# Layer 2's cross attention: who turns the outputs of its heads and their result

## The chip, the cores and the metric

One core of one Trainium2 chip runs the whole program. The metric is device time in microseconds (us), from one launch to its end. Below, PE is TensorE (PEld its weight loads), DVE is VectorE, ACT is ScalarE, POOL is GpSimd, and SP issues the DMAs.

## What is computed

Twelve blocks in four layers (cross attention, attention, feed-forward in each) add to `x`, 64 sequences of 64 tokens with 128 features. The block that changes is the first one of layer 2 (called L2x). Its queries come from `x` and its keys and values from a context of 64 x 128 tokens with 96 features:

```python
def _L2_xattn_ref(query, key_value, Wq, bq, Wk, bk, Wv, bv, Wo, bo):
    NUM_HEADS, CLAMP = 16, 10000.0
    ...
    q = (query @ Wq + bq).reshape(B, Nq, H, D).transpose(0, 2, 1, 3)
    k = (key_value @ Wk + bk).reshape(B, Nkv, H, D).transpose(0, 2, 1, 3)
    v = (key_value @ Wv + bv).reshape(B, Nkv, H, D).transpose(0, 2, 1, 3)
    attn = jnp.einsum('bhqd,bhkd->bhqk', q, k) * scale
    attn = jnp.clip(attn, -CLAMP, CLAMP)
    attn = jax.nn.softmax(attn, axis=-1)
    x = jnp.einsum('bhqk,bhkd->bqhd', attn, v).reshape(B, Nq, Cq)
    return x @ Wo + bo
...
x = x + _L2_xattn_ref(_layernorm(x, axis=-1), ctx_768, ...)
```

## The kernel before

`x` stays in SBUF through all blocks. Each block is cut into jobs of 512 tokens (L1x and L2f: 256), and two contexts, 0 and 1, work on one job each at a time. Each context has four PSUM banks, its own tiles and its own semaphores. `PLAN` says which jobs a context runs one after the other; L2x has eight jobs, four to a context.

A job is written as small programs, one or several for each engine, that yield between steps. `ORDER` is a string of some 8,300 letters; each letter lets one program of one context take its next step (a small letter is context 0, a capital context 1). `write_out` walks through it, so `ORDER` fixes the sequence of instructions on every engine, and each engine runs its own list strictly in turn. A digit in `ORDER` tells the next step to put so many filler products (`pe_warm`, L471, a 128x128 by 128x512 bf16 product whose result nobody reads) on TensorE ahead of a wait. The wait of an instruction is on semaphores that other engines raise.

A job of L2x goes like this. `pe_context`, `act_context` and `dve_L2x` make the keys (L1875, moved with bias by L1898), four masked copies of them in `kx` (two by VectorE at L1761, two by GpSimd at L2032), the values `va` (L1880, L2055), and the queries (normalised tokens turned at L463, moved at L479, multiplied at L1890, moved at L480). The values have a 17th kind of column: for each head a column of ones beside its 8 features, so that the product with the weights also gives their sum.

Then two lanes, h = 0 and 1, take eight heads each, with two of the context's four banks each. A lane makes four waves (w), each of two sequences:

1. L1969, PE: scores of 128 queries against 8 x 128 keys, in the lane's two banks.
2. L2074, L2077, L2080, DVE: maximum, its clamp, and the scores less the maximum, to `p`.
3. L2013, L2015, ACT: a Relu and the exponential, on `p`.
4. L1977, PE: eight turns of 128x128, back to the lane's banks. L2018, ACT: copy to `pT`.
5. L1985, PE: 16 products of weights and values, whose nine rows for each head land in the partitions 32n to 32n+8 of the lane's first bank.
6. L2022, ACT: copy of these 128x256 outputs to `oT`. L1992, PE: two 128x128 turns of `oT` into the lane's second bank.
7. L2083, L2086, DVE: reciprocal of the sums and the product with it, from that bank to `att`. The next wave's scores wait for this (`att`).

```python
            yield
            pe_warm(nc, j, 2 * h + 1)
            t.wait_ge(*j.at(lane_name("outT", h), w + 1))
            for g in groups:
                put = t.transpose(psum[:, 2 * h + 1, (g % 2) * P:(g % 2 + 1) * P], m["oT"][:, 0, g * P:(g + 1) * P], j.c["ident"])
            put.then_inc(*j.up(lane_name("o_turned", h)))
```

So four lanes are under way at once, two for each context, and there are 64 lane waves in all. After both lanes of a job are done, `att` (128 tokens x 128 features, four tiles) is turned by four 128x128 turns (L463), copied to `xT` (L479), multiplied by `Wo` (`pe_project`, L1387) and added to `x` (`dve_project`, L1394), which frees the context's banks (`done`).

Blocks L1a and L3x already turn their outputs in another way: `dve_divide` has VectorE turn blocks of 32x32 straight from PSUM (L1744), divide (L1747, L1750) and turn blocks again into `xT` (L1755).

## Time and profile before

| what | value |
|---|---|
| median of three runs | 2608.11 us (2601.25 to 2614.97) |
| the profiled execution's own time | 2616.77 us |
| its span | 2615.5 us |
| its mean granted TensorE clock | 0.963 of full speed |
| PE busy | 2331.4 us, 89% |
| DVE busy | 1702.6 us, 65% |
| ACT busy | 1340.3 us, 51% |
| POOL busy | 780.3 us, 30% |

Times of single instructions come from the profiled execution, which took 8.7 us longer than the median of the runs. Busy time of an engine counts each moment once, whereas the busy time of a group sums its instructions; a group's line shows the line of the kernel, engine, operation, output and inputs with their shapes, the count, the busy time and the mean, and then for how long the engine had stood idle just before these instructions and what ended that. PE busy includes the fillers and the overlap of pipelined products, so it says little by itself. The stage of L2x reaches from its first scores at 981 us to its last projection at 1288 us.

### The profile page before, as it was taken

What the parts mean: (1) busy time and instruction counts of PE and PEld (TensorE: products, weight loads), DVE (VectorE), ACT (ScalarE), POOL (GpSimd) and SP (SyncE); (2) the same over time, 40 slices, a digit from 0 to 9 for tenths busy, and PEclk for the clock granted to TensorE, in tenths of its full rate; (3) what the DMA queues carried; (4) which work ended last, traced back from release to release, by engine and by line L of the source; (5) the groups of instructions that cost most, each with busy time, mean ns of one, the idle gap of its engine ahead of it and who ended that gap; (6) DMA issues with size and microseconds to landing.
All of it is one profiled execution on the core that took longest, in us unless ns stands there. A gap on an engine that the chain in (4) does not pass through costs nothing.

```text
span 2615.5 us, 62549 instructions
## 1 busy us (share of the span) xinstructions
PE 2331.4 (89%) x26728; PEld 1560.2 (60%) x26728; DVE 1702.6 (65%) x4776; ACT 1340.3 (51%) x2305; POOL 780.3 (30%) x684
## 2 busy tenths in 40 slices
PE   5899999888889998888898888889989888999999
PEld 2566666665545555555576667666645555566666
DVE  4866556667887667768676776666776665655432
ACT  3576445776344338777754444444433566555342
POOL 2322555554121331111012233321210112454434
PEclk8999999999899999999999999999998899999999
DMA  4001442000000000000000000010010000122323
GB/s 124 14 1 37 100 105 60 22 15 11 3 3 6 1 23 37 14 14 2 11 15 19 18 19 19 27 31 14 26 55 8 8 2 2 49 53 53 106 73 89
DMA packets 50454, 84.18 MB, mean 32 GB/s; under 512 B 9536, under 2 KB 24768, under 8 KB 49792
## 3 DMA queue, kind: packets, MB, share of 16 engines
q1 hardware_dynamic: 50176, 80.18, 11.1%
q8 instruction: 210, 3.44, 0.5%
q14 instruction: 68, 0.56, 0.1%
HBM read 77.54 MB, written 2.62 MB: 31 GB/s over the span
## 4 chain that ended last, share of the span: by engine, by line
PE 55%; DVE 22%; ACT 11%; POOL 5%; issue 4%; DMA 2%; SPq 1%; DVEq 0%; POOLq 0%; ACTq 0%
PE psum L938 6%; PE psum L896 5%; PE psum L900 5%; PE psum L1598 3%; PE psum L463 2%; DVE c_L3x_most L1718 2%; PE psum L1691 2%; ACT c_L2x_p L2015 2%; PE psum L471 2%; ACT c_L2x_p L2013 2%; PE psum L1588 1%; PE psum L1387 1%; PE psum L765 1%; PE psum L770 1%; PE psum L1437 1%
## 5 line engine op out<-in xcount | busy, mean ns | idle before, releaser
L471 PE MATMUL psum<-halves_held 128*128 128x512 bf16 x616 | 177.6, 402 | 4.1 <-DVE x_held L635 2.2
L885 POOL TENSOR_TENSOR c_L3f_h<-c_L3f_h,c_L3f_spread 128x512 f32<-128x512 f32 x96 | 120.6, 1283 | 140.6 <-DMA c_L3f_spread<-scratch 107.2
L928 DVE TENSOR_TENSOR c_L3f_h<-c_L3f_h,psum 128x512 f32<-128x512 f32 (+1 forms) x112 | 75.6, 685 | 106.0 <-PE psum L900 77.9
L914 ACT ACTIVATE c_L3f_h<-psum 128x512 f32<-128x512 f32 x112 | 64.7, 594 | 108.2 <-PE psum L896 89.2
L938 PEld LDWEIGHTS psum<-weights,c_L3f_h 128*128 128x128 f32 (+1 forms) x896 | 106.7, 192 | 19.8 <-issue 16.0
L938 PE MATMUL psum<-weights,c_L3f_h 128*128 128x128 f32 (+1 forms) x896 | 109.9, 277 | 1.4 <-POOL c_L3f_h L885 1.4
L471 PEld LDWEIGHTS psum<-halves_held 128*128 128x128 bf16 x616 | 56.1, 101 | 85.1 <-issue 42.1
L896 PE MATMUL psum<-c_L3f_xT,weights 128*128 128x512 f32 x208 | 105.0, 596 | 0.0
L900 PE MATMUL psum<-c_L3f_xT,weights 128*128 128x512 f32 x208 | 104.8, 594 | 0.0
L885 POOL TENSOR_TENSOR c_L0f_h<-c_L0f_h,c_L0f_spread 128x512 f32<-128x512 f32 x64 | 80.5, 1276 | 78.3 <-DVE c_L0f_h L928 50.0
L1598 PE MATMUL psum<-c_L3x_qx,c_L3x_kT 32*128 32x256 f32 x512 | 78.8, 428 | 23.2 <-DVE c_L3x_most L1718 15.7
L2074 DVE TENSOR_REDUCE c_L2x_mx<-psum 128x8 f32<-128x1024 f32 x64 | 77.8, 1220 | 25.6 <-PE psum L1969 25.1
L885 POOL TENSOR_TENSOR c_L2f_h<-c_L2f_h,c_L2f_spread 128x256 f32<-128x256 f32 x64 | 46.4, 748 | 140.2 <-DMA c_L2f_spread<-scratch 132.8
L1977 PE MATMUL psum<-constants_held,c_L2x_p 128*128 128x128 f32 x512 | 67.7, 276 | 15.1 <-ACT c_L2x_p L2015 14.9
L2032 POOL TENSOR_TENSOR c_L2x_kx<-c_L2x_kT,constants_held 128x1024 f32<-128x1024 f32 x16 | 31.2, 1968 | 163.6 <-ACT c_L2x_kT L1898 163.6
L1718 DVE TENSOR_REDUCE c_L3x_most<-psum 128x16 f32<-128x2048 f32 x32 | 73.0, 2281 | 10.7 <-PE psum L1588 10.3
L1977 PEld LDWEIGHTS psum<-constants_held,c_L2x_p 128*128 128x128 f32 x512 | 56.5, 141 | 38.4 <-issue 25.4
L2080 DVE SCALAR_TENSOR_TENSOR c_L2x_p<-psum,c_L2x_mx 128x1024 f32<-128x1024 f32 x64 | 77.9, 1222 | 1.3
L1707 ACT ACTIVATE c_L3x_pT<-psum 128x1024 f32<-128x1024 f32 x64 | 62.5, 1021 | 25.8 <-PE psum L1620 25.6
L1598 PEld LDWEIGHTS psum<-c_L3x_qx,c_L3x_kT 32*128 32x128 f32 x512 | 47.0, 197 | 47.5 <-DVE c_L3x_most L1718 26.6
L2013 ACT ACTIVATE c_L2x_p<-c_L2x_p 128x1024 f32<-128x1024 f32 x64 | 67.7, 1058 | 14.4 <-DVE c_L2x_p L2080 14.2
L938 PEld LDWEIGHTS psum<-weights,c_L0f_h 128*128 128x128 f32 x512 | 62.5, 192 | 15.4 <-issue 12.7
(639 smaller groups left out, 6602.2 us busy)
## 6 DMA issues: line engine op xcount, KB each, us to landing
c_L0f_spread<-scratch SPq DMA_DIRECT2D x64, 256.0 KB, 5.3
c_L3f_spread<-scratch SPq DMA_DIRECT2D x32, 512.0 KB, 5.6
c_L2f_spread<-scratch SPq DMA_DIRECT2D x64, 128.0 KB, 3.0
c_L3f_spread<-scratch SPq DMA_DIRECT2D x64, 128.0 KB, 6.1
c_L0x_ctxT<-ctxT SPq DMA_DIRECT2D x8, 384.0 KB, 4.8
c_L1x_ctx<-ctx SPq DMA_DIRECT2D x16, 192.0 KB, 2.4
c_L2x_ctxT<-ctxT SPq DMA_DIRECT2D x8, 384.0 KB, 3.6
c_L3x_ctxT<-ctxT SPq DMA_DIRECT2D x8, 384.0 KB, 3.5
```

Source lines behind the costliest of these rows:

```text
L471: nc.tensor.matmul(j.psum[:, bank, :], j.half["ident"], j.half["take"], start=True, stop=True)
L885: nc.gpsimd.tensor_tensor(h, h, j.m["spread"][:, f, :], ALU.mult).then_inc(*j.up("mixed"))
L896: t.matmul(psum[:, 1 + 2 * f % 3, 0:j.tok], j.weight("gate")[:, cols], m["xT"][:], start=True, stop=True).then_inc(*j.up("gate"))
L900: t.matmul(psum[:, 1 + (2 * f + 1) % 3, 0:j.tok], j.weight("up")[:, cols], m["xT"][:], start=True, stop=True).then_inc(*j.up("inner"))
L928: nc.vector.tensor_tensor(h, h, j.psum[rows, bank, 0:j.tok], ALU.mult).then_inc(*j.up("gated"))
L938: put = nc.tensor.matmul(j.psum[:, 0, k * P:(k + 1) * P], j.m["h"][rows, f, k * P:(k + 1) * P], j.weight("down")[rows, f * P:(f + 1) * P], ...
L1598: nc.tensor.matmul(j.psum[rows, g, at:at + 256].rearrange("p (j q) -> p j q", j=QUAD), j.m["kT"][f, s * keys:(s + 1) * keys], j.m["qx"][f, ...
L1718: put = v.tensor_reduce(m["most"][:, u, :].rearrange("p (g j) -> p g j", j=QUAD), psum[:, :, u * QUAD * keys:(u + 1) * QUAD * keys].rearra ...
L1977: put = t.transpose(psum[:, n // 4, (n % 4) * P:(n % 4 + 1) * P], m["p"][:, n * P:(n + 1) * P], j.c["ident"])
L2013: s.activation(p, p, ACT.Relu, scale=-1.0).then_inc(*j.up(lane_name("e_low", h)))
L2074: v.tensor_reduce(mx, s, AX, ALU.max).then_inc(*j.up(lane_name("max", h)))
L2080: v.scalar_tensor_tensor(p, s, -limit, bcast(mx, 2, SC), ALU.max, ALU.subtract).then_inc(*j.up(lane_name("low", h)))
```

## The change

In L2x the steps 6 and 7 are written in another way, as in `dve_divide`:

- ScalarE's copy (L2022) and TensorE's two turns (L1992) of each lane wave go. VectorE turns the 128x256 outputs in 32x32 blocks from PSUM into `oT` (new L2075), and the reciprocal and the product now read `oT`.
- The products of weights and values (new L1984) write each sequence's 64 columns as two pieces of 32, so that a block turn puts each token where it belongs.
- At the end of a job TensorE's four turns of `att` and ScalarE's copy of them go. VectorE turns `att` (128x512) in 32x32 blocks into `xT` (new L2047). The rows of `Wo` are laid out to match (`by_lane`).
- The next wave's scores wait for `o_turned` in place of `att`.
- In `pe_linear` of L2a, TensorE also waits for the `done` of the context's job before (`free_bank`).
- All of `ORDER` is new; `PLAN` is as it was.

```diff
--- before.py
+++ after.py
@@ -113,7 +113,7 @@
         ("lb", P, 512, lambda a: a["L1_ffn_lora_B"].transpose(0, 2, 1).reshape(P, 512))]
     t["L2x"] = [
         ("wq", P, P, lambda a: a["L2_xattn_Wq"]), ("wk", CX, P, lambda a: a["L2_xattn_Wk"]),
-        ("wv", CX, P, lambda a: a["L2_xattn_Wv"]), ("wo", P, P, lambda a: a["L2_xattn_Wo"]),
+        ("wv", CX, P, lambda a: a["L2_xattn_Wv"]), ("wo", P, P, lambda a: by_lane(a["L2_xattn_Wo"])),
         ("bq", P, 1, lambda a: col(a["L2_xattn_bq"])), ("bk", P, 1, lambda a: col(a["L2_xattn_bk"])),
         ("bv", P, P, lambda a: row(a["L2_xattn_bv"])), ("bo", P, P, lambda a: row(a["L2_xattn_bo"]))]
     t["L2a"] = [
@@ -650,6 +650,8 @@
             put = t.matmul(psum[:, bank, n * P:(n + 1) * P], m["xT"][:, n * P:(n + 1) * P], j.weight(w), start=True, stop=True)
         put.then_inc(*j.up("keys"))
     yield
+    if heads == 16:
+        j.free_bank(t)
     pe_warm(nc, j, 3)
     t.wait_ge(*j.at("values", 1))
     t.wait_ge(*j.at("kx", 1))
@@ -1938,12 +1940,8 @@
     t, m, psum = nc.tensor, j.m, j.psum
     yield from pe_context(nc, j)
     yield
-    t.wait_ge(*j.at("att", j.tiles))
-    t.wait_ge(*j.at("att_b", j.tiles))
-    pe_turn(nc, j, 0, m["att"])
-    yield
-    pe_warm(nc, j, 2)
-    t.wait_ge(*j.at("features", 2))
+    pe_warm(nc, j, 1)
+    t.wait_ge(*j.at("mixed", 1))
     pe_project(nc, j, 2, m["xT"])
 
 
@@ -1956,8 +1954,8 @@
         for w in range(j.tiles):
             yield
             if w:
-                pe_warm(nc, j, 2 * h)
-                t.wait_ge(*j.at(lane_name("att", h), w))
+                pe_warm(nc, j, 2 * h + 1)
+                t.wait_ge(*j.at(lane_name("o_turned", h), w))
             else:
                 t.wait_ge(*j.at("q_ready", 1))
                 t.wait_ge(*j.at("va", 1))
@@ -1982,24 +1980,16 @@
                 for r in range(2):
                     for n in range(QUAD):
                         col = (QUAD * g + n) * P + r * S
-                        put = t.matmul(psum[LANE * n:LANE * n + ONE, 2 * h, (g % 2) * P + r * S:(g % 2) * P + (r + 1) * S],
-                                       m["va"][:, 2 * w + r, QUAD * g + n, :], m["pT"][:, col:col + S], start=True, stop=True)
+                        out = psum[LANE * n:LANE * n + ONE, 2 * h, r * P:(r + 1) * P].rearrange("p (b c) -> p b c", b=2)
+                        put = t.matmul(out[:, :, (g % 2) * LANE:(g % 2 + 1) * LANE], m["va"][:, 2 * w + r, QUAD * g + n, :],
+                                       m["pT"][:, col:col + S].rearrange("p (b c) -> p b c", b=2), start=True, stop=True)
             put.then_inc(*j.up(lane_name("out", h)))
-            yield
-            pe_warm(nc, j, 2 * h + 1)
-            t.wait_ge(*j.at(lane_name("outT", h), w + 1))
-            for g in groups:
-                put = t.transpose(psum[:, 2 * h + 1, (g % 2) * P:(g % 2 + 1) * P], m["oT"][:, 0, g * P:(g + 1) * P], j.c["ident"])
-            put.then_inc(*j.up(lane_name("o_turned", h)))
 
     return program
 
 
 def act_L2x(nc, j):
     yield from act_context(nc, j)
-    yield
-    nc.scalar.wait_ge(*j.at("turned", 2))
-    act_turned(nc, j, j.m["xT"][:], 0).then_inc(*j.up("features"))
 
 
 def act_lane_L2x(h):
@@ -2017,9 +2007,6 @@
             s.wait_ge(*j.at(lane_name("p_turned", h), w + 1))
             s.copy(m["pT"][:, h * 1024:(h + 1) * 1024].rearrange("p (a b) -> p a b", a=2),
                    psum[:, 2 * h:2 * h + 2, :]).then_inc(*j.up("pT1" if h else "pT0"))
-            yield
-            s.wait_ge(*j.at(lane_name("out", h), w + 1))
-            s.copy(m["oT"][:, 0, 256 * h:256 * h + 256], psum[:, 2 * h, 0:256]).then_inc(*j.up(lane_name("outT", h)))
 
     return program
 
@@ -2054,6 +2041,10 @@
     v.wait_ge(*j.at("values", 1))
     v.tensor_tensor(m["va"][:, :, :, 0:WIDTH], psum[:, 2:4, :].rearrange("p a (s h d) -> p (a s) h d", s=4, h=HEADS),
                     bcast(j.weight("bv").rearrange("p (h d) -> p h d", h=HEADS), 1, j.seqs), ALU.add).then_inc(*j.up("va"))
+    yield
+    v.wait_ge(*j.at("att", j.tiles))
+    v.wait_ge(*j.at("att_b", j.tiles))
+    v.transpose(m["xT"][:], m["att"][:].rearrange("p t d -> p (t d)")).then_inc(*j.up("mixed"))
     yield
     v.wait_ge(*j.at("biased", 1))
     dve_project(nc, j, 2)
@@ -2067,7 +2058,8 @@
         p = m["p"][:, h * 1024:(h + 1) * 1024].rearrange("p (n k) -> p n k", k=SC)
         s = psum[:, 2 * h:2 * h + 2, :].rearrange("p a (n k) -> p (a n) k", k=SC)
         mx, z = m["mx"][:, h * 8:(h + 1) * 8], m["z"][:, 0, h * 8:(h + 1) * 8]
-        out = psum[:, 2 * h + 1, 0:256].rearrange("p (h e) -> p h e", h=8)
+        out = m["oT"][:, 0, 256 * h:256 * h + 256]
+        blocks = out.rearrange("p (b g c) -> p b g c", b=4, g=2)
         for w in range(j.tiles):
             yield
             v.wait_ge(*j.at(lane_name("scores", h), w + 1))
@@ -2079,12 +2071,16 @@
             v.wait_ge(*j.at(lane_name("max", h), 2 * w + 2))
             v.scalar_tensor_tensor(p, s, -limit, bcast(mx, 2, SC), ALU.max, ALU.subtract).then_inc(*j.up(lane_name("low", h)))
             yield
+            v.wait_ge(*j.at(lane_name("out", h), w + 1))
+            v.transpose(out, psum[:, 2 * h, 0:256]).then_inc(*j.up(lane_name("o_turned", h)))
+            yield
             v.wait_ge(*j.at(lane_name("o_turned", h), w + 1))
-            v.reciprocal(z, out[:, :, WIDTH]).then_inc(*j.up(lane_name("denom", h)))
+            v.reciprocal(z, lane_blocks(out)[:, :, WIDTH]).then_inc(*j.up(lane_name("denom", h)))
             yield
             v.wait_ge(*j.at(lane_name("denom", h), w + 1))
-            v.tensor_tensor(m["att"][:, w, 64 * h:64 * h + 64].rearrange("p (h d) -> p h d", h=8), out[:, :, 0:WIDTH],
-                            bcast(z, 2, WIDTH), ALU.mult).then_inc(*j.up(lane_name("att", h)))
+            att = m["att"][:, w, :].rearrange("p (b h g d) -> p b h g d", b=4, h=2, g=2)[:, :, h]
+            v.tensor_tensor(att, blocks[:, :, :, 0:WIDTH], bcast(z.rearrange("p (b g) -> p b g", b=4), 3, WIDTH),
+                            ALU.mult).then_inc(*j.up(lane_name("att", h)))
 
     return program
 
@@ -2844,76 +2840,75 @@
 ORDER = (
-    "qQddDDpdDlLdkqddDKDpdVPavagpAlGdPapAgppPvvDaAvkvDvpPaPLqdGQpDadPdKlpVVgaApgVppvvdVaVPAPvQkGADvvpPapDgAqdPaddDGPLplDKPaVV"
...
+    "qQDdDdDdpLldDkqdKQDVpvPadaDgDpPaAgpALpGpPvdvlaAvGdvvpPakgPqpPdaDdKpVVdaApgVlpVVPPApDAGDPvvDadkvAGLvvpPapDgqdPQadpPaKpVdV"
...
```

`by_lane` and `free_bank` were there before:

```python
def by_lane(w):
    return np.ascontiguousarray(w.reshape(4, 4, 8, w.shape[1]).transpose(1, 0, 2, 3)).reshape(P, w.shape[1])
...
    def free_bank(self, engine):
        if not self.first:
            self.free(engine)
```

What the new `ORDER` makes of the lists is best seen in three places. First TensorE where both contexts pass from their second to their third job of L2x. L1387 (now L1389) is a job's projection, L1875 and L1880 (now L1877 and L1882) the keys and values of the next, L1969 (L1967) scores, L1977 (L1975) the turns of `p`, L1985 (L1984) weights by values. Before:

```order
L463 MATMUL psum<-constants_held,c_L2x_att 128x128 x8
L471 MATMUL psum<-halves_held 128x512 x3
L1387 MATMUL psum<-weights,c_L2x_xT 128x128 x4
L1875 MATMUL psum<-c_L2x_ctxT,weights 128x512 x2
L1880 MATMUL psum<-weights,c_L2x_ctxT 128x128 x8
L463 MATMUL psum<-constants_held,c_L2x_xn 128x128 x4
L1387 MATMUL psum<-weights,c_L2x_xT 128x128 x4
L1875 MATMUL psum<-c_L2x_ctxT,weights 128x512 x2
L471 MATMUL psum<-halves_held 128x512
L1890 MATMUL psum<-c_L2x_xT,weights 128x512
L1880 MATMUL psum<-weights,c_L2x_ctxT 128x128 x8
```

And now:

```order
L1389 MATMUL psum<-weights,c_L2x_xT 128x128 x4
L1984 MATMUL psum<-c_L2x_pT,c_L2x_va 9x2x32 x16
L471 MATMUL psum<-halves_held 128x512
L1967 MATMUL psum<-c_L2x_kx,c_L2x_qT 64x512 x4
L471 MATMUL psum<-halves_held 128x512
L1975 MATMUL psum<-constants_held,c_L2x_p 128x128 x8
L1984 MATMUL psum<-c_L2x_pT,c_L2x_va 9x2x32 x16
L471 MATMUL psum<-halves_held 128x512 x3
L1967 MATMUL psum<-c_L2x_kx,c_L2x_qT 64x512 x4
L1877 MATMUL psum<-c_L2x_ctxT,weights 128x512 x2
L1882 MATMUL psum<-weights,c_L2x_ctxT 128x128 x8
L471 MATMUL psum<-halves_held 128x512
```

Before, the two projections stood four rows of the list apart, with the keys and values of the one between them; now they stand fifteen rows apart, and between them the other context's lanes go on (the second projection is four rows below this piece). Counted over the stage, the pairs stand 12, 4 and 12 rows apart before and 29, 15 and 30 now; the last pair is one row of eight products in both.

Second, VectorE in the middle of a job, where L2083 and L2086 are now L2078 and L2082, L2074, L2077 and L2080 are L2066, L2069 and L2072, and L2075 is new. Before:

```order
L2083 RECIPROCAL c_L2x_z<-psum 128x8
L2086 TENSOR_TENSOR c_L2x_att<-psum,c_L2x_z 128x64
L2074 TENSOR_REDUCE c_L2x_mx<-psum 128x8
L2077 TENSOR_SCALAR c_L2x_mx<-c_L2x_mx 128x8
L2080 SCALAR_TENSOR_TENSOR c_L2x_p<-psum,c_L2x_mx 128x1024
L2083 RECIPROCAL c_L2x_z<-psum 128x8
L2086 TENSOR_TENSOR c_L2x_att<-psum,c_L2x_z 128x64
L2074 TENSOR_REDUCE c_L2x_mx<-psum 128x8
L2077 TENSOR_SCALAR c_L2x_mx<-c_L2x_mx 128x8
```

And now:

```order
L2072 SCALAR_TENSOR_TENSOR c_L2x_p<-psum,c_L2x_mx 128x1024
L409 TENSOR_SCALAR c_L2x_norm_rstd<-c_L2x_norm_moments 128x4
L2075 STREAM_TRANSPOSE c_L2x_oT<-psum 128x256
L2078 RECIPROCAL c_L2x_z<-c_L2x_oT 128x8
L2082 TENSOR_TENSOR c_L2x_att<-c_L2x_oT,c_L2x_z 128x4x16
L2066 TENSOR_REDUCE c_L2x_mx<-psum 128x8
L2069 TENSOR_SCALAR c_L2x_mx<-c_L2x_mx 128x8
L2072 SCALAR_TENSOR_TENSOR c_L2x_p<-psum,c_L2x_mx 128x1024
```

The pair of reciprocal and product has become three instructions, with the block turn at their head, and it stands between the subtraction of one lane and the maximum of another, as it did.

Third, TensorE's fillers (L471) within the lanes. Before:

```order
L1985 MATMUL psum<-c_L2x_pT,c_L2x_va 9x64 x16
L471 MATMUL psum<-halves_held 128x512 x7
L1977 MATMUL psum<-constants_held,c_L2x_p 128x128 x8
L1985 MATMUL psum<-c_L2x_pT,c_L2x_va 9x64 x16
L471 MATMUL psum<-halves_held 128x512
L1977 MATMUL psum<-constants_held,c_L2x_p 128x128 x8
L1992 MATMUL psum<-constants_held,c_L2x_oT 128x128 x4
L1985 MATMUL psum<-c_L2x_pT,c_L2x_va 9x64 x32
```

And now:

```order
L471 MATMUL psum<-halves_held 128x512 x3
L1967 MATMUL psum<-c_L2x_kx,c_L2x_qT 64x512 x4
L471 MATMUL psum<-halves_held 128x512 x9
L1975 MATMUL psum<-constants_held,c_L2x_p 128x128 x8
L471 MATMUL psum<-halves_held 128x512 x4
L1975 MATMUL psum<-constants_held,c_L2x_p 128x128 x8
L1984 MATMUL psum<-c_L2x_pT,c_L2x_va 9x2x32 x16
L471 MATMUL psum<-halves_held 128x512 x2
L1967 MATMUL psum<-c_L2x_kx,c_L2x_qT 64x512 x4
```

The rows with L1992 are gone, and rows of fillers stand ahead of most turns and scores. From the first to the last row of L2x there were 187 fillers and are now 315; outside it there were 429 and are 408. Apart from what is named above, the number and the forms of the instructions are the same on every engine.

## Rows read from the trace of the kernel before

**Rows 1.** Windows: stretch, its length, then busy us and (count) of each engine, clock.
```profile
core 0: us, PE busy (x) PEld busy (x) DVE busy (x) ACT busy (x) POOL busy (x), PEclk, DMA share, GB/s
981.00:1288.00 307.00, 271.55 (x3645) 158.58 (x3645) 225.86 (x416) 242.98 (x317) 43.65 (x29) 0.99 0.04 14
1000.00:1040.00 40.00, 36.88 (x591) 21.40 (x579) 31.10 (x58) 37.92 (x53) 0.00 (x0) 1.00 0.01 2
1120.00:1140.00 20.00, 18.27 (x195) 12.54 (x183) 7.72 (x22) 9.18 (x14) 7.71 (x4) 1.00 0.14 41
1140.00:1150.00 10.00, 8.37 (x42) 3.68 (x42) 9.84 (x21) 6.68 (x8) 3.22 (x4) 0.83 0.00 0
600.00:800.00 200.00, 168.25 (x3444) 105.46 (x3443) 158.46 (x382) 89.95 (x168) 50.25 (x38) 0.92 0.02 4
```

**Rows 2.** Groups by line, VectorE, 980 to 1290 us: count, busy us, mean ns, idle before.
```profile
L2074 DVE TENSOR_REDUCE c_L2x_mx<-psum 128x8 f32<-128x1024 f32 x64 | 77.8, 1220 | 25.6 <-PE psum L1969 25.1
...
L2086 DVE TENSOR_TENSOR c_L2x_att<-psum,c_L2x_z 128x64 f32<-128x64 f32 x64 | 13.5, 220 | 1.3
L2083 DVE RECIPROCAL c_L2x_z<-psum 128x8 f32<-128x8 f32 x64 | 12.6, 201 | 38.6 <-PE psum L1992 37.9
```

**Rows 3.** Groups by line, ScalarE, the same stretch.
```profile
L2022 ACT COPY c_L2x_oT<-psum 128x256 f32<-128x256 f32 x64 | 22.8, 368 | 8.2 <-PE psum L1985 7.7
...
L479 ACT COPY c_L2x_xT<-psum 128x512 f32<-128x512 f32 x15 | 8.6, 585 | 16.6 <-PE psum L463 16.6
```

**Rows 4.** Groups by line, TensorE, the same stretch.
```profile
L471 PE MATMUL psum<-halves_held 128*128 128x512 bf16 x187 | 53.9, 392 | 1.9 <-DVE c_L2x_p L2080 1.9
...
L1992 PE MATMUL psum<-constants_held,c_L2x_oT 128*128 128x128 f32 x128 | 25.5, 291 | 5.3 <-ACT c_L2x_oT L2022 4.8
...
L463 PE MATMUL psum<-constants_held,c_L2x_att 128*128 128x128 f32 x32 | 4.9, 282 | 2.1 <-DVE c_L2x_att L2086 1.9
```

**Rows 5.** The chain of waits, 1000 to 1040 us, shares by line.
```profile
by line: ACT c_L2x_p L2015 21.2%; ACT c_L2x_p L2013 19.3%; ACT c_L2x_pT L2018 16.0%; ACT c_L2x_xn L424 7.7%; PE psum L1969 7.6%; PE psum L1977 7.5%; PE psum L1985 6.8%; ACT c_L2x_oT L2022 4.2%; PE psum L471 4.0%; PE psum L1992 3.5%; issue 1
```

**Rows 6.** One line each, VectorE: min/median/max ns, first and last start, form.
```profile
L1744 DVE STREAM_TRANSPOSE c_L3x_oT<-psum x32: 682/717/718, 1787.3 to 2186.8; 128x512 f32<-128x512 f32 x32
L1744 DVE STREAM_TRANSPOSE c_L1a_oT<-psum x16: 1207/1250/1251, 654.8 to 833.5; 128x1024 f32<-128x1024 f32 x16
...
L1755 DVE STREAM_TRANSPOSE c_L3x_xT<-c_L3x_att x32: 254/311/313, 1788.6 to 2188.2; 128x128 f32<-128x128 f32 x32
L1755 DVE STREAM_TRANSPOSE c_L1a_xT<-c_L1a_att x16: 431/445/446, 659.1 to 835.6; 128x256 f32<-128x256 f32 x16
```

**Rows 7.** One line each, TensorE: products of weights and values.
```profile
L1691 PE MATMUL psum<-c_L3x_pT,c_L3x_va x2048: 218/219/315, 1786.1 to 2186.5; 128*9 128x64 f32 x187
...
L1985 PE MATMUL psum<-c_L2x_pT,c_L2x_va x2048: 218/219/226, 993.4 to 1284.9; 128*9 128x64 f32 x187
```

**Rows 8.** Timeline, the end of one lane's wave: start us, duration us, engine, line.
```profile
1163.85 0.63 PE L1985 MATMUL psum<-c_L2x_pT,c_L2x_va 128*9 128x64 f32 x32
...
1164.55 0.37 ACT L2022 COPY c_L2x_oT<-psum 128x256 f32<-128x256 f32 x1
...
1164.97 0.44 PE L1992 MATMUL psum<-constants_held,c_L2x_oT 128*128 128x128 f32 x2 [0.17 <-ACT c_L2x_oT L2022]
...
1165.45 0.21 DVE L2083 RECIPROCAL c_L2x_z<-psum 128x8 f32<-128x8 f32 x1 [1.27 <-PE psum L1992]
```

**Rows 9.** Timeline, the end of a job, 1201 to 1205 us.
```profile
1201.73 0.35 DVE L2086 TENSOR_TENSOR c_L2x_att<-psum,c_L2x_z 128x64 f32<-128x64 f32 x2
...
1202.23 0.63 PE L463 MATMUL psum<-constants_held,c_L2x_att 128*128 128x128 f32 x4 [0.78 <-DVE c_L2x_att L2086]
1202.89 0.58 ACT L479 COPY c_L2x_xT<-psum 128x512 f32<-128x512 f32 x1
...
1203.53 1.16 PE L1387 MATMUL psum<-weights,c_L2x_xT 128*128 128x128 f32 x8 [0.68 <-ACT c_L2x_xT L479]
```

**Rows 10.** Timeline, a run of five filler products.
```profile
1170.76 1.24 PE L471 MATMUL psum<-halves_held 128*128 128x512 bf16 x5
```

137 lines of the change are left out of this document (68 added, 69 removed).

## The prediction

> **What bounds the kernel now.** I read first where the stage that changes lies and how full each engine is in it. L2x takes 307 us, from 981 to 1288 us of the span. In it ScalarE is busy for 243.0 us (79%), VectorE for 225.9 us (74%) and TensorE for 271.6 us (88%), its fillers included [rows 1]. No engine is full over the whole stage, but the stage has two kinds of stretches. While all four lanes run, as from 1000 to 1040 us, ScalarE is busy for 37.92 of 40 us, 94.8%, and VectorE for 31.10, 78% [rows 1]. The chain of waits says the same there: its largest shares are ScalarE's Relu, exponential and copy of `pT` (19.3, 21.2 and 16.0%); the copy that the change removes has 4.2% and TensorE's turns of it 3.5% [rows 5]. Where both contexts pass to their next job at nearly the same time, as from 1120 to 1140 us, ScalarE is busy for 9.2 of 20 us and VectorE for 7.7 [rows 1]: the time goes to projection, keys and queries. So L2x is bound by ScalarE with holes at the changes of jobs.
>
> Next I read what the steps to be removed cost their engines, and who waits at them. The copies of the outputs are 64 x 368 ns, 22.8 us on ScalarE; those of the result and of the tokens together are 15 in the window, 585 ns each [rows 3]. TensorE's turns of the outputs are 25.5 us, those of `att` 4.9 us [rows 4]. VectorE has stood idle for 38.6 us ahead of the 64 reciprocals, nearly all of it until those turns had ended, and for 25.6 us ahead of the maxima [rows 2]. That is the room into which new work on VectorE can go without lengthening anything.
>
> **The change, part by part.** *ScalarE* loses 22.8 us, and 8 copies of 585 ns, 4.7 us [rows 3]. It keeps 243.0 - 27.5 = 215.5 us.
>
> *VectorE* gains two kinds of turns, and L2x has neither now. The trace has such turns in other blocks: from PSUM, 128x512 takes 717 ns and 128x1024 takes 1250 ns (medians), from SBUF 128x128 takes 311 and 128x256 takes 445 ns [rows 6]. From PSUM an element costs (1250 - 717)/512 = 1.04 ns, so 128x256 should take 717 - 266 = 451 ns, and 64 of them 28.9 us. From SBUF it is (445 - 311)/128 = 1.05 ns, so 128x512 should take 445 + 268 = 713 ns, and 8 of them 5.7 us. The bounds for the first are 311 ns (as small as the smallest turn there is) and 717 ns (as long as the next larger one): 20 to 46 us. I take the value on the line, since two rows of the same form give it. The reciprocals (201 ns) and products (220 ns) [rows 2] read SBUF in place of PSUM and keep their sizes; I change nothing there. VectorE then needs 225.9 + 34.6 = 260.5 us. It becomes the fullest of the three beside TensorE, and is about where ScalarE is now with 243.0.
>
> The Trainium skill, in VectorE: DVE Perf Modes, section The TRN2 errata, gives an operation from PSUM on VectorE 120 cycles and one for each element, at 0.96 GHz; for 256 elements that would be 392 ns and an estimated 25.1 us in place of 28.9, and the stage below would come out some 4 us shorter. For 512 elements it would give 658 ns where the row has 717, so the row decides.
>
> *TensorE* loses 25.5 + 4.9 = 30.4 us [rows 4]. It gets 128 more fillers in the stage (315 against 187). In a run they take 1.24 us for five [rows 10], so some 0.21 to 0.25 us each once one has begun, and 53.9/187 = 0.29 us by the group's line [rows 4]: 27 to 37 us. That is the same room again. Where they stand ahead of a wait that lasts anyway they cost nothing; the cover is ScalarE's Relu and exponential, or VectorE's steps. If that cover were gone they would cost their own length (a rival, below). The products of weights by values write two pieces of 32 columns; L3x, which does so now, has a median of 219 ns as has L2x [rows 7], so 0.
>
> *The path of one lane* grows shorter. The last output of a wave is done at 1164.48 us; copy, hand-over and turns bring the reciprocal to 1165.45 us, 0.97 us later [rows 8]. With a hand-over of 0.07 us, as the copy has, a turn of 0.45 us and 0.03 us to the next instruction it would be 0.55 us: 0.42 us less, and a lane has 16 waves, 6.7 us. At the end of a job the last product ends at 1202.08 us and the projection starts at 1203.53 us, 1.45 us [rows 9]; a turn of 0.71 us and a hand-over take 0.8: 0.6 us less, four times in a context, 2.5 us. Together 9 us, if nothing queued anywhere. What is queued behind the new turn on VectorE is another lane's maximum; it stood behind the reciprocal in the same place before, which waited for an event 0.8 us later.
>
> *Changes of jobs* lie further apart in the new list (29, 15 and 30 rows between the two projections of a pair, where there were 12, 4 and 12). Then two lanes of the other context go on, and the hole from 1120 to 1140 us [rows 1], where VectorE is idle for 12.3 us, should be partly filled, three times.
>
> *The wait for* `done` *in L2a*: 0. The addition that raises it stands ahead of the new job's keys on VectorE's list, and these same products wait for the keys already.
>
> *The order outside L2x* is new as well, with no instruction changed but 21 fillers fewer, some 5 us of TensorE. No row says what a new order is worth there. From 600 to 800 us, for example, the granted clock is 0.92 [rows 1], and 8% of 200 us is 16 us that could go or come back elsewhere; I take 0 and keep 12 us to both sides.
>
> *The sum.* The stage's length is the need of its fullest engine over the share it reaches. ScalarE reaches 79.1% over the stage and 94.8% in a stretch with four lanes [rows 1]. VectorE with 260.5 us would take 329 us at the first share and 275 us at the second: 22 us more or 32 us less than 307. I take the middle, 87%, since the holes get smaller but don't go: 260.5/0.87 = 299 us, 8 us less. It agrees with the 9 us of the path. Against the profiled execution of 2616.8 us that is 2609 us; this lies 8.7 us above the median of the runs, so against the median it is 2608.1 - 8 = 2600 us. Half a percent, 13 us, is about what a measurement of this kernel can tell from no change: faster means below 2595 us, slower above 2621 us. The share at which nothing is gained is 260.5/307 = 84.9%.
>
> **The rivals.**
>
> *A, the holes close.* VectorE reaches 91%, because the job changes no longer fall together and the freed ScalarE is always ahead. For it: the spacing in TensorE's list, and the 64 us that VectorE waits now [rows 2]. Against it: where VectorE is fuller than ScalarE now, from 600 to 800 us, it is at 158.46/200 = 79% [rows 1]. It gives 260.5/0.91 = 286 us, 21 us less: 2587 us.
>
> *B, VectorE becomes the bound and packs badly.* Each lane wave now needs it three times, for subtraction and maximum and now for a turn that another engine could do beside. Its list is strict, so a turn that waits for late products holds the next lane's maximum, and ScalarE's freed 27.5 us are spent waiting. It decides below a share of 84.9%; at ScalarE's present 79.1% the stage takes 329 us, 22 us more: 2630 us. Against it: that share comes from holes which the list now spaces out. The Trainium skill, in VectorE: DVE Perf Modes, section Specifications, speaks against the change in the same way: VectorE sits closer to SBUF and ScalarE closer to PSUM, and here a read of PSUM moves from ScalarE's 368 ns to an expected 451 ns, so by the rule both new figures land on the wrong engine.
>
> *C, the fillers hold.* TensorE's list gives back 27 to 37 us for 30.4 us saved. If they stand where no wait is, TensorE needs up to 271.6 - 30.4 + 37 = 278 us, at its present 88.5% [rows 1] 314 us: 7 us more, 2615 us. Too few of them could let the clock fall, as from 1140 to 1150 us, where the granted clock is 0.83, so for a part at 1.2 GHz; over the stage it is 0.99 [rows 1], so more fillers have little to win back.
>
> *D, the order elsewhere decides*, by 12 us or more to either side: 2588 or 2612 us and beyond. This is also the case in which the change doesn't do what it says: L2x moves by its 8 us, and the total shows something else.
>
> **How the numbers follow.** The forecast has 0.42, with a range of its own from 2591 to 2609 us; A 0.25, B 0.17, C 0.07, D 0.09. Faster by over 13 us: all of A (0.25), the lower end of the forecast (0.07) and half of D (0.04), 0.36. Slower: nearly all of B (0.16) and a little of C and D (0.03), 0.19. Within: 0.45. The range from 2575 to 2626 us takes in A with the skill of its order, C, most of D and the milder half of B; outside remain the worse half of B and the far ends of A and D, near 0.2.
>
> **What would show it right or wrong.** Turns of 128x256 near 0.45 us and of 128x512 near 0.71 us, 64 and 8 of them. L2x shorter by some 8 us; VectorE at 260 us in it and above 85% of it, ScalarE at 215 us. The largest wait on VectorE should be at the turn, for the products of weights by values, and be less than the 38.6 us at the reciprocal now. The chain of waits in the middle of L2x should run through VectorE's maximum and subtraction instead of ScalarE's three steps. If L2x takes over 307 us with VectorE waiting at its turns, B is right; if TensorE's turns start later than the exponentials end, behind fillers, C; if L2x is 299 us and the total far from 2600 us, D.

## The result, and the profile after

The changed kernel takes 2675.34 us in the median of four runs (2672.96 to 2676.44) against 2607.66 us for the one before: a ratio of 1.0266, with an interval from 1.0244 to 1.0289. It is 68 us slower. The forecast was 2600 us and the range ended at 2626 us; the side was wrong, and so was the range.

The profiled execution took 2672.96 us (span 2671.6 us, clock 0.962), against 2616.77 us before. From the start and end of each block's rows on TensorE one sees where the difference of the two spans, 56 us, lies:

| rows of TensorE, us | before | after |
|---|---|---|
| first of L2x | 967.6 | 970.9 |
| last of L2x | 1290.1 | 1346.8 |
| so L2x has | 322.5 | 375.9 |
| from there to the last row of all | 1322.3 | 1321.8 |

53 of 56 us are in L2x, 3 ahead of it, none behind. The medians differ by 68 us, 12 more than the two profiled executions: that of before took 9 us more than its median, that of the change 2 us less. Where those 12 us lie no run shows. The windows of the changed kernel, to set beside [rows 1]; the first is the whole of L2x, the second the stretch that the prediction measured (first scores to last projection, there 307 us, now 364), the others are from its middle:

```profile
core 0: us, PE busy (x) PEld busy (x) DVE busy (x) ACT busy (x) POOL busy (x), PEclk, DMA share, GB/s
971.00:1347.00 376.00, 305.56 (x3704) 169.26 (x3702) 269.11 (x513) 229.93 (x257) 55.62 (x36) 0.96 0.04 13
983.00:1347.00 364.00, 293.56 (x3637) 160.74 (x3629) 262.33 (x502) 225.32 (x249) 45.75 (x30) 0.96 0.04 14
1100.00:1140.00 40.00, 34.65 (x509) 18.29 (x507) 27.94 (x58) 33.05 (x38) 0.00 (x0) 1.00 0.01 2
1180.00:1220.00 40.00, 33.27 (x471) 17.34 (x472) 31.47 (x66) 28.49 (x32) 1.02 (x1) 1.00 0.00 1
```

VectorE has 262.3 us of work, where 260.5 were forecast, but in 364 us: 72% of it, where 87% were taken and 79.1% was the low bound. And while before there were stretches with ScalarE at 94.8%, now four lanes run and neither engine is full: from 1180 to 1220 us VectorE is busy for 31.47 and ScalarE for 28.49 of 40 us.

Set against the 322.5 us of before, where VectorE was busy for 234.0 us between the same two rows of TensorE, the stage is 53 us longer: VectorE has 35 us more of work and stands idle for 107 us in place of 88. The added work has not gone into the idle time, and 18 us more of idling have come on top.

Groups by line in 971 to 1347 us, to set beside [rows 2 to 4]:

```profile
L2075 DVE STREAM_TRANSPOSE c_L2x_oT<-psum 128x256 f32<-128x256 f32 x64 | 28.4, 446 | 72.9 <-PE psum L1984 72.5
L2066 DVE TENSOR_REDUCE c_L2x_mx<-psum 128x8 f32<-128x1024 f32 x64 | 77.8, 1217 | 14.4 <-PE psum L1967 14.0
L2082 DVE TENSOR_TENSOR c_L2x_att<-c_L2x_oT,c_L2x_z 128x64 f32<-128x64 f32 x64 | 13.8, 222 | 1.2
L2078 DVE RECIPROCAL c_L2x_z<-c_L2x_oT 128x8 f32<-128x8 f32 x64 | 12.1, 196 | 1.1
L2047 DVE STREAM_TRANSPOSE c_L2x_xT<-c_L2x_att 128x512 f32<-128x512 f32 x8 | 5.6, 705 | 0.8 <-issue 0.4
L2003 ACT ACTIVATE c_L2x_p<-c_L2x_p 128x1024 f32<-128x1024 f32 x64 | 67.6, 1056 | 75.1 <-DVE c_L2x_p L2072 74.7
L2008 ACT COPY c_L2x_pT<-psum 128x1024 f32<-128x1024 f32 x64 | 64.3, 1006 | 34.2 <-PE psum L1975 34.2
L471 PE MATMUL psum<-halves_held 128*128 128x512 bf16 x315 | 84.3, 390 | 13.7 <-DVE c_L2x_p L2072 13.7
```

The new instructions have their forecast lengths (446 and 705 ns). What is new is in the last column: VectorE stands idle for 72.9 us ahead of its turns, until the products of weights and values are there (38.6 us ahead of the reciprocals before), and ScalarE for 75.1 us ahead of the Relu, until VectorE has subtracted. In the kernel before, that second wait was 14.4 us (L2003 was L2013 there):

```profile
L2013 ACT ACTIVATE c_L2x_p<-c_L2x_p 128x1024 f32<-128x1024 f32 x64 | 67.7, 1058 | 14.4 <-DVE c_L2x_p L2080 14.2
```

The chain of waits, 1100 to 1140 us, by line. It led through three steps of ScalarE before [rows 5]; now VectorE's subtraction and maximum are its largest shares, and ScalarE's three have 21% together:

```profile
by line: DVE c_L2x_p L2072 20.9%; DVE c_L2x_mx L2066 20.7%; PE psum L1967 11.0%; ACT c_L2x_p L2003 8.0%; ACT c_L2x_p L2005 8.0%; PE psum L1975 7.7%; PE psum L471 5.1%; ACT c_L2x_pT L2008 5.1%; PE psum L1984 4.6%; DVE c_L2x_mx L2069 3.1%; DV
```

How it comes to that is seen in the timeline (start, duration, engine, line, and in brackets the idle time before):

```profile
1187.11 1.23 DVE L2072 SCALAR_TENSOR_TENSOR c_L2x_p<-psum,c_L2x_mx 128x1024 f32<-128x1024 f32 x1
...
1188.37 1.06 ACT L2003 ACTIVATE c_L2x_p<-c_L2x_p 128x1024 f32<-128x1024 f32 x1 [0.19 <-DVE c_L2x_p L2072]
...
1188.93 0.45 DVE L2075 STREAM_TRANSPOSE c_L2x_oT<-psum 128x256 f32<-128x256 f32 x1 [0.52 <-PE psum L1984]
...
1190.60 1.23 DVE L2066 TENSOR_REDUCE c_L2x_mx<-psum 128x8 f32<-128x1024 f32 x1 [0.71 <-PE psum L1967]
...
1190.66 1.06 PE L1975 MATMUL psum<-constants_held,c_L2x_p 128*128 128x128 f32 x8
...
1191.76 1.01 ACT L2008 COPY c_L2x_pT<-psum 128x1024 f32<-128x1024 f32 x1 [1.25 <-PE psum L1975]
...
1192.06 1.23 DVE L2072 SCALAR_TENSOR_TENSOR c_L2x_p<-psum,c_L2x_mx 128x1024 f32<-128x1024 f32 x1
...
1192.83 0.63 PE L1984 MATMUL psum<-c_L2x_pT,c_L2x_va 128*9 128x64 f32 x32
...
1193.53 0.45 DVE L2075 STREAM_TRANSPOSE c_L2x_oT<-psum 128x256 f32<-128x256 f32 x1 [0.25 <-PE psum L1984]
```

A lane is subtracted by 1188.34 us; Relu, exponential, turns, copy and products take till 1193.46 us, 5.1 us, and only then can VectorE turn its outputs. In between VectorE's list has one other lane's turn, reciprocal and product, its maximum and its subtraction: some 3.6 us of work. The rest it waits, and ScalarE has one lane's wave in hand at a time. I call a turn **early** if on VectorE's list it stands behind at most one other lane's subtraction since its own. For the kernel before one counts the reciprocal, which stood in its place. Of the 64 lane waves 21 are early before, and 48 are after. The trace says that most of the waiting is theirs: of the 73 us ahead of the turns, 56.8 are at the 48 early ones.

### The profile page after: what moved, and what is told of

It is laid out like the page before. It is cut to its first block, busy times and chain, and to the rows that moved or that the text cites. A ratio compares the mean times of both kernels' runs of the same rounds, so it can differ in the third digit from the quotient of the medians.

```text
span 2671.6 us, 62423 instructions
## 1 busy us (share of the span) xinstructions
PE 2348.2 (88%) x26675; PEld 1556.6 (58%) x26675; DVE 1741.7 (65%) x4848; ACT 1320.4 (49%) x2233; POOL 784.2 (29%) x684
## 4 chain that ended last, share of the span: by engine, by line
PE 51%; DVE 25%; ACT 9%; issue 7%; POOL 5%; DMA 1%; SPq 1%; DVEq 0%; POOLq 0%; ACTq 0%
PE psum L940 6%; PE psum L902 4%; PE psum L898 4%; PE psum L1600 3%; PE psum L463 2%; DVE c_L2x_p L2072 2%; DVE c_L2x_mx L2066 2%; PE psum L1693 2%; PE psum L1975 2%; PE psum L471 1%; DVE c_L3x_most L1720 1%; PE psum L1590 1%; PE psum L1389 1%; PE psum L1967 1%; PE psum L1439 1%
## 5 line engine op out<-in xcount | busy, mean ns | idle before, releaser
L471 PE MATMUL psum<-halves_held 128*128 128x512 bf16 x723 | 200.8, 395 | 15.8 <-DVE c_L2x_p L2072 13.7
L471 PEld LDWEIGHTS psum<-halves_held 128*128 128x128 bf16 x723 | 64.4, 100 | 113.8 <-issue 39.7
L916 ACT ACTIVATE c_L3f_h<-psum 128x512 f32<-128x512 f32 (+1 forms) x112 | 64.7, 594 | 122.8 <-PE psum L898 100.8
L2003 ACT ACTIVATE c_L2x_p<-c_L2x_p 128x1024 f32<-128x1024 f32 x64 | 67.6, 1056 | 75.1 <-DVE c_L2x_p L2072 74.7
L1975 PE MATMUL psum<-constants_held,c_L2x_p 128*128 128x128 f32 x512 | 73.3, 290 | 16.9 <-ACT c_L2x_p L2005 16.0
L2066 DVE TENSOR_REDUCE c_L2x_mx<-psum 128x8 f32<-128x1024 f32 x64 | 77.8, 1217 | 14.4 <-PE psum L1967 14.0
L1975 PEld LDWEIGHTS psum<-constants_held,c_L2x_p 128*128 128x128 f32 x512 | 59.5, 147 | 46.0 <-ACT c_L2x_p L2005 27.8
L2008 ACT COPY c_L2x_pT<-psum 128x1024 f32<-128x1024 f32 x64 | 64.3, 1006 | 34.2 <-PE psum L1975 34.2
L1967 PE MATMUL psum<-c_L2x_kx,c_L2x_qT 32*64 32x512 f32 x512 | 62.5, 612 | 18.2 <-DVE c_L2x_oT L2075 9.4
L2072 DVE SCALAR_TENSOR_TENSOR c_L2x_p<-psum,c_L2x_mx 128x1024 f32<-128x1024 f32 x64 | 77.5, 1215 | 1.3
L2075 DVE STREAM_TRANSPOSE c_L2x_oT<-psum 128x256 f32<-128x256 f32 x64 | 28.4, 446 | 72.9 <-PE psum L1984 72.5
```

What stands on the lines that cost most here:

```text
L471: nc.tensor.matmul(j.psum[:, bank, :], j.half["ident"], j.half["take"], start=True, stop=True)
L1967: put = t.matmul(psum[64 * r:64 * r + 64, g, :].rearrange("p (j k) -> p j k", j=QUAD), m["qT"][f, s * S:(s + 1) * S], m["kx"][f, :, s * SC ...
L1975: put = t.transpose(psum[:, n // 4, (n % 4) * P:(n % 4 + 1) * P], m["p"][:, n * P:(n + 1) * P], j.c["ident"])
L2066: v.tensor_reduce(mx, s, AX, ALU.max).then_inc(*j.up(lane_name("max", h)))
L2072: v.scalar_tensor_tensor(p, s, -limit, bcast(mx, 2, SC), ALU.max, ALU.subtract).then_inc(*j.up(lane_name("low", h)))
```

## The experiments

Each experiment's time stands against runs of the kernel before on the same chip, in the same series; the ratio is the one to them, with its interval of 95%. In the diffs of `ORDER` one line stands for the whole string.

**The old order with the changed program.** The letters of the removed steps are dropped from the `ORDER` of before, and the turn's letter is put ahead of the reciprocal's. The program is that of the change.

```diff
-... MxZnWy4nYmWdWxNDXzzDLmnwwGmYzkNzzMY4NXwyMZZw ...
+... MxZnWYmWdWNDXzzzDLnwwwGmYzkNzzMXwyMZZZw1NwZn ...
```

> The changed program with the order of before: every step of L2x that still exists keeps its old place, the removed steps (ScalarE's copies, TensorE's turns) are left out with their 61 fillers, VectorE's turn of the outputs stands just ahead of its reciprocal, and its turn of the result where TensorE's turn of it stood. Theory O (the new order packs L2x badly; the turns themselves are cheap): 2595 to 2612 us, no slower than before, L2x about 300 to 310 us. Theory V (the turns load VectorE until it is the bound, whatever the order): 2650 to 2680 us, L2x above 355 us, VectorE's idle time ahead of its turns near the 73 us of the changed kernel.

It takes 2630.81 us (2625.55 to 2638.87; ratio 1.0079, 1.0052 to 1.0107), and a further run of the same kernel, below, 2626.34 us. So some 45 of the 68 us go when the order alone is put back. That lies between the two theories, and so does the stage: 336.3 us by TensorE's rows, where they had 310 at most or over 355.

```profile
967.00:1303.00 336.00, 263.97 (x3502) 155.41 (x3503) 266.38 (x509) 225.55 (x252) 50.40 (x33) 0.93 0.05 15
```

```profile
L2003 ACT ACTIVATE c_L2x_p<-c_L2x_p 128x1024 f32<-128x1024 f32 x64 | 67.6, 1057 | 43.0 <-DVE c_L2x_p L2072 42.6
...
L2075 DVE STREAM_TRANSPOSE c_L2x_oT<-psum 128x256 f32<-128x256 f32 x64 | 27.9, 437 | 19.6 <-PE psum L1984 19.6
```

VectorE has the same work as in the change and does it in 40 us less: it waits 19.6 us at its turns instead of 72.9. Against the kernel before, this one is still 19 us slower; its clock in L2x is 0.93 where that had 0.99, and ScalarE waits 43.0 us ahead of the Relu where it waited 14.4.

**The new order with the program of before.** At the place of VectorE's turn stand ScalarE's copy and TensorE's turns; at the end of a job likewise. Reciprocal and product had to be brought forward too, ahead of the lane's next scores, which wait for them in this program.

```diff
- "qQddDDpdDlLdkqddDKDpdVPavagpAlGd ...
+ "qQDdDdDdpLldDkqdKQDVpvPadaDgDpPa ...
```

> The program of before with the new order: where VectorE's turn stood, ScalarE's copy and TensorE's turns follow each other, and reciprocal and product are brought forward to stand ahead of the next scores of their lane. Theory O: slow without any turn on VectorE, 2665 us or more (each wave has a longer path, 64 x 0.4 us would give 2700 us). Theory V: near 2608 us, up to 2620 us.

2798.27 us in two runs (ratio 1.0728, 1.0689 to 1.0767), with L2x from 978.8 to 1467.2 us, 488 us. VectorE waits (970 to 1460 us) at the reciprocals until TensorE's turns are done:

```profile
L2083 DVE RECIPROCAL c_L2x_z<-psum 128x8 f32<-128x8 f32 x62 | 12.6, 205 | 166.9 <-PE psum L1992 166.9
```

Theory O had 2665 us or more. This order is bad for the old program too, and worse; that one's way from subtraction to reciprocal is longer by a copy and the turns. So an order like this loses without any turn on VectorE, and the two runs together put the larger part of the loss, 45 of 68 us, on the order. How much of the 190 us here comes from the places of reciprocal and product, which are not those of the change, no run separates. This run has the new order in all blocks; L2x starts 8 us later than in the change, and is 112 us longer.

**Fillers of the change cut**, in L2x from 315 to 130.

```diff
-... dyVww1nAVPywGxnPz1nzzAmz1PxzdzlmGw3myVwwwA ...
+... dyVwwnAVPywGxnPznzzAmzPxzdzlmGw1myVwwwA ...
```

> The changed kernel, each filler count within L2x halved and rounded down (130 fillers in place of 315). Theory F (fillers hold TensorE's real work back in L2x): 185 fewer at 0.21 us, up to 40 us back, 2635 to 2650 us. Theories O and V: they fill waits that last anyway, 2665 to 2680 us, or a little slower if the granted clock falls in L2x.

2701.96 us (2688.66 and 2715.25; ratio 1.0359, 1.0291 to 1.0427) against the 2675 us of the change. Theory F had 2635 to 2650 us; the others had 2680 us at most, or a little more if the clock fell, and it did. The granted clock in L2x falls from 0.96 to 0.88 and L2x gets longer, 387 us:

```profile
964.00:1351.00 387.00, 290.14 (x3515) 165.24 (x3515) 268.60 (x513) 230.06 (x258) 55.58 (x36) 0.88 0.04 13
```

On balance the fillers don't hold the lanes up: with 185 fewer TensorE's turns take 318 ns a piece in place of 290, and none of the up to 40 us comes back that theory F expected. Rival C is out.

**The old order, once more.** The kernel is the same as in the first experiment.

> placeholder label kept apart: the same kernel as e1_old_order, one more look at it beside the three below, to see how far one profile of it differs from another. All theories: 2625 to 2640 us.

2626.34 us. It shows how far two profiles of one kernel lie apart. By TensorE's rows L2x takes 341.9 us here, from 964.0 to 1305.9, and 336.3 in the first experiment, with the clock at 0.90 and 0.93:

```profile
964.00:1306.00 342.00, 267.35 (x3478) 160.80 (x3505) 266.65 (x510) 225.45 (x252) 50.40 (x33) 0.90 0.05 15
```

The other engines' work is the same. So where two kernels have one profile each, as below, a difference of up to some 6 us in the length of the stage tells nothing.

**The old order, fillers kept.** The 60 fillers that stood ahead of the removed steps go to the lane's next step on TensorE.

```diff
-... WNDXzzzDLnwwwGmYzkNzzMXwyMZZZw1NwZn ...
+... WNDXzzzDL4nwwwGmYzkNzzMXwyMZZZw5NwZ ...
```

> e1_old_order, but the 60 fillers of the removed steps are given to the lane's next step on TensorE. Theory K (the 19 us by which e1_old_order is over the kernel before are the clock, granted 0.93 in its L2x against 0.99): 2605 to 2618 us with the clock in L2x back above 0.97. Theory V (what is left of it is VectorE's added work): 2625 us or more, clock back or not.

2623.77 us (2620.36 to 2632.69; ratio 1.0050, 1.0031 to 1.0068). The clock of L2x is 0.95 in place of 0.93, its length 338 us, no shorter than without. Theory K asked for a clock above 0.97, which these fillers don't give, and the time lies between the two theories. So more fillers are no cure there; what the full 0.99 would give back is not shown.

**L2x packed anew, both programs.** The steps of L2x (and some 80 letters at each side) are put into a new order, made from the durations and waits in the traces with the aim of the least waiting on VectorE and ScalarE; it was done in the same way for the changed program and for that of before, each with its own steps. All else is as in the old order.

```diff
-... pVaVVVpVdvlVVVgpaVVVVVpVvPvgpAVPgpV ...
+... pVaVgpalggvVVppVVVGVPVpVVPVVVVVpVLd ...
```

> The changed program; outside L2x the order of before, inside it an order packed anew by hand of the durations in the traces, so that VectorE and ScalarE are waited for least, with 121 fillers in the gaps left. Theory O (only the order was bad): L2x shorter than the 322 us of before, 2575 to 2600 us. Theory V: no order gets it under 2608 us. If the clock falls (fewer gaps are filled, 121 fillers against 187), 2600 to 2625 us.

> The program of before with an L2x order packed in the same way, 145 fillers. Theory O' (the kernel before had slack of its own; the turns on VectorE are worth what the programs differ by when both are packed alike): 2590 to 2610 us, some 15 us over e7_new_program_packed. Theory V: it is the faster of the two.

The changed program takes 2615.01 us (10 runs, ratio 1.0018, 0.9999 to 1.0036), the program of before 2609.93 us (10 runs, 1.0008, 0.9982 to 1.0033). Of the changed program's 64 turns 29 are early; VectorE waits 27.1 us at them, and L2x takes 326.9 us, 49 us less than in the change. In the program of before it is 327.7 us. The 2575 to 2600 us of theory O did not come; what came is the third case, 2600 to 2625 us with a fallen clock (0.88 in the stage). Nor is the changed program ahead of the old one by 15 us: the two are level.

The count of early turns is not the whole account either. The packed order has 29 of them and 27.1 us of waiting there, more than the old order's 21 and 19.6, and its stage is 9 us shorter; ScalarE waits 19.0 us ahead of the Relu where it waited 43.0.

**More fillers in the packed orders.** 220 and 278 in L2x in place of 121, for the changed program; 298 in place of 145 for that of before.

```diff
-... dyxPVwwwYNyzzz2mZZZWwWMwWnm2mwwNNnwwZz3NZz ...
+... dyxPVwwwYNyzzz4mZZZWwWMwW2nm4mwwNNnwwZz5NZz ...
```

> The packed order of the changed program again, with 220 filler products inside layer 2's cross attention in place of 121; nothing else differs. Packed before, the stage took 327 us at a granted clock of 0.88, and the kernel stood at 1.0018 of the one before. If the clock is what still holds it (at 0.88 a set of eight turns took 302 ns apiece in the mean), the clock of the stage goes to 0.93 or more, the stage to 315 to 322 us and the kernel to 2603 to 2610 us. If fillers that start in a gap hold up the product that comes behind them (0.22 us each at full clock), the clock rises all the same and the stage stays at 327 us or gets up to 10 us longer.

> The same again with 278 fillers in the stage. By the clock: 0.95 or more, the stage 312 to 320 us. By fillers in the way: longer than with 220, by up to 58 x 0.27 = 16 us.

> The program of before in its own packed order, with 298 fillers in the stage in place of 145 (it ran at 1.0008 with a clock of 0.93 in the stage). It is the fair partner of the two runs above: if the change of program is worth something once both are packed and fed alike, the better of those two beats this one by over 0.3%; if the change is worth nothing, they agree within 0.3%. By the clock this one comes out at 2600 to 2608 us; by fillers in the way at 2612 to 2625 us.

Over 11 runs each: 2611.73 us with 220 (ratio 0.9990, 0.9967 to 1.0012), 2629.97 us with 278 (1.0063, 1.0041 to 1.0086), and 2624.82 us for the old program with 298 (1.0049, 1.0028 to 1.0070). The windows of L2x with 121 and with 220 fillers:

```profile
961.00:1288.00 327.00, 271.30 (x3435) 157.38 (x3471) 271.68 (x509) 223.33 (x249) 50.88 (x32) 0.88 0.05 15
```

```profile
961.00:1288.00 327.00, 280.84 (x3573) 159.63 (x3572) 272.17 (x508) 224.11 (x249) 50.88 (x32) 0.93 0.05 15
```

The clock of the stage rises, its length stays at 326.9 us. So of the two cases set down for 220 fillers the one of the clock (315 to 322 us) failed, and the one of fillers in the way came. At 278 fillers the stage is 330.6 us, 4 more, which is within what two profiles differ by, but the whole kernel is 18 us slower. The old program's stage goes from 327.7 to 335.8 us with 298 fillers, again the case of fillers in the way.

By the rule set down beforehand, that the better of the two changed kernels beat this one by over 0.3%, the change of program would be worth something: 0.9990 against 1.0049. But the old program is better with 145 fillers, at 1.0008, and set against that the difference is 0.2% with intervals that overlap. The best version of the changed program is thus level with the kernel before (2611.22 us over 27 runs), and no version of either program is shown to be faster than it.

**Turns moved up.** The test of the mechanism itself: the kernel of the first experiment, where on VectorE's list alone the turn, reciprocal and product of 33 lane waves are moved up. 54 of 64 turns are early now, where 21 were (46 stand behind just one other lane's subtraction, as 33 do in the change, and 8 behind none). TensorE's and ScalarE's lists are the same. One place of VectorE's list:

```diff
 L2072 SCALAR_TENSOR_TENSOR c_L2x_p<-psum,c_L2x_mx 128x1024
+L2075 STREAM_TRANSPOSE c_L2x_oT<-psum 128x256
+L2078 RECIPROCAL c_L2x_z<-c_L2x_oT 128x8
+L2082 TENSOR_TENSOR c_L2x_att<-c_L2x_oT,c_L2x_z 128x4x16
 L2066 TENSOR_REDUCE c_L2x_mx<-psum 128x8
 L2069 TENSOR_SCALAR c_L2x_mx<-c_L2x_mx 128x8
```

> The changed program in the order of before (2630.81 us) with one thing altered: on VectorE's list, the turn, reciprocal and product of 33 of the 64 lane waves are moved up, to right behind one other lane's subtraction instead of behind two or more, so that 46 of 64 stand as 33 do in the change. TensorE's and ScalarE's lists are the same. If what costs in the change is that VectorE comes to the turn before its products are ready, the idle time before the turns rises from 19.6 us to 60 us or more, and the kernel gets longer by 30 to 90 us. If VectorE's load alone is the cost, nothing is added to it, and the time stays within 10 us of 2630.

2739.10 us (2732.28 to 2747.79; ratio 1.0470, 1.0440 to 1.0500): 108 us more than without the move, above the top of what I expected. Not a microsecond of work is added to VectorE, and L2x grows from 336 to 456 us:

```profile
967.00:1423.00 456.00, 323.57 (x3502) 190.76 (x3503) 270.62 (x509) 227.21 (x252) 49.97 (x33) 0.74 0.04 11
```

```profile
L2003 ACT ACTIVATE c_L2x_p<-c_L2x_p 128x1024 f32<-128x1024 f32 x64 | 67.6, 1057 | 137.9 <-DVE c_L2x_p L2072 137.8
...
L2075 DVE STREAM_TRANSPOSE c_L2x_oT<-psum 128x256 f32<-128x256 f32 x64 | 28.4, 443 | 143.5 <-PE psum L1984 143.5
```

The wait at the turns grows by 123.9 us and the stage by 120; 141.4 of the 143.5 us are at the 54 early turns. The timeline has the pattern of the change, drawn larger:

```profile
1051.52 1.22 DVE L2072 SCALAR_TENSOR_TENSOR c_L2x_p<-psum,c_L2x_mx 128x1024 f32<-128x1024 f32 x1
1052.78 1.06 ACT L2003 ACTIVATE c_L2x_p<-c_L2x_p 128x1024 f32<-128x1024 f32 x1 [1.31 <-DVE c_L2x_p L2072]
...
1054.83 0.99 ACT L2008 COPY c_L2x_pT<-psum 128x1024 f32<-128x1024 f32 x1
...
1055.88 1.04 PE L1984 MATMUL psum<-c_L2x_pT,c_L2x_va 128*9 128x64 f32 x32 [0.41 <-ACT c_L2x_pT L2008]
1056.99 0.45 DVE L2075 STREAM_TRANSPOSE c_L2x_oT<-psum 128x256 f32<-128x256 f32 x1 [4.25 <-PE psum L1984]
```

Here VectorE comes to the turn right after a subtraction and sits still for 4.25 us. The clock falls to 0.74 as well, with TensorE busy for 71% of the stage where it was 79%, and TensorE's turns take 353 ns a piece for 284: part of the 120 us is slower products. The test shows that places of the turns alone can cost so much; it goes further than the change does (54 early turns for 48), so its 108 us are no measure of the change's share.

**Work added to one engine.** Last, what the work of each engine is worth in the packed order with 220 fillers. In one kernel VectorE makes each turn twice, the first time into a spare tile; in the other ScalarE makes an extra 128x256 copy ahead of that of the turned weights.

```diff
+            v.transpose(m["oT2"][:, 256 * h:256 * h + 256], psum[:, 2 * h, 0:256])
             v.transpose(out, psum[:, 2 * h, 0:256]).then_inc(*j.up(lane_name("o_turned", h)))
```

```diff
             s.wait_ge(*j.at(lane_name("p_turned", h), w + 1))
+            s.copy(m["oT2"][:, 256 * h:256 * h + 256], psum[:, 2 * h, 0:256])
             s.copy(m["pT"][:, h * 1024:(h + 1) * 1024].rearrange("p (a b) -> p a b", a=2),
```

> The packed changed program with 220 fillers (2611.73 us), where VectorE makes the turn of each lane wave twice, the first time into a spare tile: 64 x 442 ns = 28.3 us more of VectorE's work in the stage, and 16 x 0.44 = 7 us more on any one lane's own way. If VectorE is what bounds the packed stage (it was at work for about 83% of it), 20 to 28 us are added. If the lanes' own ways bound it, about 7 us. If neither does, under 5 us.

> The same kernel, where ScalarE instead makes an extra 128x256 copy from PSUM ahead of each copy of the turned weights: 64 x 368 ns (the size of the copy that the change removed) = 23.6 us more of ScalarE's work, and 5.9 us on one lane's own way. The prediction took ScalarE as the engine whose work counts: by that 15 to 24 us are added, and about as much was to be won by the removal. If VectorE has become the bound, ScalarE's extra work costs less than half of what VectorE's does in the run beside it: 0 to 10 us.

With VectorE's turns doubled: 2617.12 us (6 runs, 2609.07 to 2629.81; ratio 1.0029, 0.9999 to 1.0060), 5 us more than the 2611.73 without; by the ratios, each to its own series, 10 us. With ScalarE's extra copy: 2630.38 us (4 runs, 2628.00 to 2632.93; ratio 1.0076, 1.0056 to 1.0095), 19 us more, by the ratios 22. In L2x itself it is -1.3 us for the first (325.6 us against 326.9) and 7 us for the second (333.9). The rest of the second's lies where nothing differs: its profiled execution is 28 us longer than that with 220 fillers, 13 of them ahead of L2x, with a clock of 0.94 in place of 0.97 up to 960 us, and 8 behind it. The windows, VectorE's first:

```profile
961.00:1290.00 329.00, 278.96 (x3599) 159.57 (x3599) 291.29 (x574) 226.13 (x255) 52.25 (x34) 0.95 0.05 15
```

```profile
965.00:1308.00 343.00, 287.31 (x3611) 164.29 (x3610) 275.42 (x515) 245.71 (x323) 57.13 (x37) 0.94 0.05 15
```

VectorE does 291.3 us of work in 329, 88.5%, and the stage isn't a microsecond longer for it: the doubled turns go into waits (16.7 us are left ahead of them, from 26.8, and 7.6 ahead of the maxima, from 14.7). The 20 to 28 us that a bound on VectorE had forecast did not come, neither in the stage nor in the kernel. So in the packed order VectorE is not the bound even with 19 us more than the change gives it. ScalarE's work costs 7 us in the stage for 23.5 added. That is near the 5.9 us on a lane's own way and hardly more than two profiles differ by. In the whole kernel it costs more than VectorE's; the runs with the same mean clock, 0.961, took 2628.00 us with the copy and 2616.37 without, so some 12 us, from one run each on different chips.

## Why the prediction was wrong

**The step that failed** is the share that the fullest engine reaches: "I take the middle, 87%, since the holes get smaller but don't go". The share was 72%, below the low end of 79.1% that I had kept for the range. VectorE's work ahead of it in the sum was right, and the share multiplied all of it: 262.3 us of VectorE's work over 0.87 are 301 us, over 0.72 the 364 us that were measured. I had treated the share as a property of the stage, between two values seen with the old order. It is one of the order. With the same program it was 79% in the old order, 83% packed, 72% in the changed one and 59% with the turns moved up; none of them reached 0.87 (the 88.5% with doubled turns has more work in the same time). Besides, both values were ScalarE's, and the sum divided VectorE's work by them. VectorE's own share before was 225.86 of 307 us, 74% [rows 1], near the 72% that came. The same holds for what I said of VectorE's waits, "the room into which new work on VectorE can go without lengthening anything": in the old order VectorE idles for 70 us of the stage, where it idled for 88, so part of the new work did go into waits; in the changed order none did (107 us).

**I read the wrong sign of the order.** I counted how far the changes of jobs lay apart and took them for the holes to be closed. What I should have counted as well was next to it in the lists that I had before me: how many other lanes' subtractions stand between a lane's own and its turn. It went from 21 to 48 early ones out of 64, and a lane's way of 5.1 us against 3.6 us of other work says that an early turn waits. Moving only this, in the old order, cost 108 us, and going back to the old order gave back 45. How much of those 45 us comes from the turns' places and how much from the rest of the order (the spacing of jobs among it) no run separates.

**VectorE's list**, "it stood behind the reciprocal in the same place before": what I said of the maximum held for the one place that I had looked at, and not over the stage.

**Rival B** had the mechanism, "a turn that waits for late products holds the next lane's maximum, and ScalarE's freed 27.5 us are spent waiting", and the trace shows both halves: 72.9 us ahead of the turns, 75.1 us ahead of the Relu. It had the wrong size, 22 us where the same stretch grew by 57 (from 307 to 364), since its share too came from the old order, and too small a chance, 0.17. It also had half of its name wrong: it was the packing, not VectorE's load, as the doubled turns show. What I set against it, that the list spaced the holes out, was no evidence.

**What held.** The turns: 446 ns for 451, 705 for 713. VectorE's work: 262.3 us for 260.5. ScalarE has 225.3 us in the stage where 215.5 were forecast. Its groups sum up to 255.8 us before and 230.8 after, 25.0 less and near the 27.5; but a window counts each moment once, and there the 255.8 were 243.0 and the 230.8 are 225.3, so a part of the short copies had run beside other instructions and their removal frees less. The wait for `done` costs nothing that shows: behind L2x both kernels take 1322 us. The fillers: rival C is refuted, since cutting fillers cost time. The clock in the stage went from 0.99 to 0.96, with more fillers than before. Rival D, the order elsewhere, is not what decided: 3 us ahead of L2x and none behind by the two profiles, though the 12 us that these leave unplaced are of the size that D had. The Trainium skill's sentence in VectorE: DVE Perf Modes, section The TRN2 errata, would have made the turn from PSUM 392 ns; the runs show 446, so the rows were the better guide. Its 658 ns for 512 elements hold for PSUM too, and the change's turn of 512 elements, 705 ns, reads SBUF; the row to set beside them has 717 ns [rows 6]. Its rule in section Specifications, VectorE closer to SBUF and ScalarE to PSUM, has 446 ns here against ScalarE's 368 on its side [rows 3], but that cost was not what made the change slow.

**Why the gain did not come even when packed.** The forecast had 8 us, from the share of 87%, and saw them borne out by a lane's path that is 9 us shorter. Packed in the same way, the changed program stands at 0.9990 to 1.0018 and that of before at 1.0008; L2x is 326.9 and 327.7 us. So in these orders the change of program is worth some 0.3% at most either way; one packing of each program doesn't show what the best order of each would give. Why ScalarE's shorter work brings nothing stays open. Putting about as much of it back cost 7 us in the stage, near the forecast size, but in an order made for less; that the old program does without this loss because its order is its own is argued, not shown.

## What to carry to other kernels

Where each engine runs a strict list, a step that waits for another engine's long way needs enough independent work ahead of it on its own list: write down the way (here 5.1 us) and the work that the list puts in between (3.6 us), and count over the whole stage how often it falls short. The count warns, it doesn't price: the packed order has more such turns than the old one and is no slower. A new order and a new program are two changes; price them one by one: here the order lost some 45 us, where the program was to win 8. And an engine's share of a stage is no constant to divide by: it belongs to the order that it was read from.

## What the runs showed of the hardware

The granted clock differs between runs of one kernel, and the time goes with it. The packed kernel with 220 fillers took 2603.12 and 2603.25 us with a mean clock of 0.967, 2611.96 with 0.962, 2620.02 with 0.955 and 2626.97 with 0.954. L2f, which has the same instructions in the same order in all orders kept from before, took 533 us in one kernel (the packed program of before, clock 0.98) and 553 in another (the packed changed program with 278 fillers, 0.95). This needs no difference between kernels: the two profiles of the one kernel in the old order have it too, the first experiment's first and the further run's second:

```profile
1373.00:1926.00 553.00, 481.26 (x8092) 366.11 (x8089) 370.90 (x1097) 240.13 (x430) 147.24 (x181) 0.95 0.08 22
```

```profile
1375.00:1913.00 538.00, 466.19 (x8075) 356.28 (x8094) 369.36 (x1099) 239.81 (x430) 146.78 (x181) 0.97 0.08 23
```

The other engines' busy time is the same to 2 us. For this kernel, then, a difference of half a percent between two orders can be clock in a block that neither touches.

The 18 us by which 278 fillers are slower than 220 are another matter, since the medians over 11 runs each differ by them. In the profiled executions 16 of 23 us lie behind the stage, with the lower clock in L2f. But runs with like clocks differ as well: 2614.02 us at 0.969 with 278 fillers and 2608.32 at 0.968 with 220, 2629.97 at 0.960 and 2615.08 at 0.960. So the mean clock alone doesn't account for the 18 us, and where the rest lies no run here settles.
